# Four transformer stages on one core: the maximum pass of the softmax cut into pairs of units on 64 rows each, with four shared banks

## Chip, core and metric

One NeuronCore of a Trainium2 chip runs the whole program in one launch. The metric is the device time in microseconds; the kernel before has a median of 374.66 us over three runs (373.7 to 376.79).

## What is computed

Two layers work on x of 4 batches x 512 positions x 128 channels, with a context of 154 keys a batch. Each layer is a gated cross attention with a gated feed-forward part behind it; the first feed-forward part is quantised, the second is a recurrence over the batches.

```python
x = x + tanh(g_xattn[0]) * L0_xattn(layernorm(x), ctx, ctx, ...)      # 16 heads of 8
x = x + tanh(g_ffn[0])   * L0_ffn(layernorm(x), ...)                  # 16-bit activations, 4-bit weights
x = x + tanh(g_xattn[1]) * L1_xattn(layernorm(x), ctx, ctx, ...)      # the same with a causal mask
x = x + tanh(g_ffn[1])   * L1_ffn(layernorm(x), ...)                  # c = f*c + i*g, h = tanh(...)
# in both attentions:
attn = softmax(einsum('bhqd,bhkd->bhqk', q, k) / sqrt(8), axis=-1)
out = einsum('bhqk,bhkd->bhqd', attn, v)
```

## The kernel before, in words

**Two passes over the scores.** The softmax takes the exponential of a score less its row's maximum, and scores are computed twice. The maximum pass (`scores_for_top`, L870) computes them with queries on the partitions and keys along the free axis, so that VectorE can reduce over keys (`take_top`, L1184). The negated maxima are split into two parts (`split_top`, L1192), transposed by TensorE (`turn_top`, L894), copied by ScalarE (`copy_top`, L702) and sent by two transfers of the SP queue into spare rows of the query tile. The second pass (`scores`, L903) computes keys x queries, with the maximum subtracted by those rows, ScalarE takes the exponential (`exps`, L709), and `weigh` (L928) multiplies by the values on four strips of 32 columns of the array at once.

**Rows of a tile.** The query tile Q4 has, on its partitions, four blocks j of 32 rows, one for each head of a group g; each block holds the high and low parts of a head's query. Kd is block diagonal in the same way: the keys of head j have only the 32 rows of block j filled. One matmul over 128 rows thus gives up to four heads, each from 32 rows.

**Units.** `max_units` cuts the 64 combinations of query tile (4 of 128 positions) and head (16) of a batch into units that fill a PSUM bank: three heads of 154 keys, 462 columns; in layer 1 the first query tile sees at most 128 keys, and its units are four heads of 128. There are 22 units a batch in layer 0 and 20 in layer 1. A unit that crosses a group of four heads is two matmuls (`parts`). In layer 1 each matmul of the first two query tiles has a mask matmul behind it (L889, an identity times a mask). All these matmuls use the whole array and the type fp32r, one instruction each; fp32 products take two.

**The order of work is written out by hand.** For each layer, i runs from -1 to 4, and each i has 20 slots. In a slot TensorE does one score tile of batch i, then the units that `units_at` gives it (of batch i+1 in slots 0 to 12, first ones of batch i+2 in slots 17 to 19), then what PE_PLAN lists: rounds of `weigh` (slots 7, 10, 13, 17, and the tails at 1 and 3 of the next i), the transposes of normed rows (`turn_normed`, L857), the query projection (`project_q`, L865), `turn_top` at slot 14, the output projection at 8. VectorE and ScalarE follow lists of their own with the same slots. Each engine runs its instructions in order, so a wait stops all that is behind it. At i = -1 there are no score tiles: all units of batch 0 are made, and the first eight of batch 1.

**PSUM.** Two banks are for score tiles, two for the weighted values, three in a ring for units (unit k waits until VectorE has reduced unit k-3), and one, `misc`, for all small products in turn; `fill_misc` waits until the one before has been read out. The feed-forward parts use the same banks under other names.

**Low parts of q.** `q_low` on VectorE computes the low part of the first two batches' queries straight from the bank; at i = -1 the second one stands at slot 6 (SECOND_QLOW_AT).

**Rank-1 bias.** `outputs_x` (L974) adds a bias row by matmuls one row deep (L982), between full matmuls.

## Time and profile before

| | |
|---|---|
| median of three runs | 374.66 us |
| profiled execution: time, span | 375.1 us, 373.0 us |
| TensorE matmuls (PE) | 285.1 us busy, 76% |
| TensorE weight loads (PEld) | 167.8 us, 45% |
| VectorE (DVE) | 251.6 us, 67% |
| ScalarE (ACT) | 182.5 us, 49% |
| GpSimd (POOL) | 125.0 us, 34% |
| mean granted clock of TensorE | 0.897 |
| reductions of the maximum pass (L1188) | 168, 97.2 us |
| matmuls of the maximum pass (L885), masks (L889) | 240, 74.2 us; 48, 13.5 us |
| score matmuls (L913) | 128, 60.2 us |

Busy times are of one profiled execution. The ends of matmuls are modelled in the trace and consecutive ones overlap, so a mean duration of a matmul (383 ns for L885) is more than what it adds to a chain of them; differences between ends show that. The granted clock is a share of full speed: 1.0 is 2.4 GHz, 0.5 is 1.2 GHz.

### The profile page before, as it was taken

The page shows a single profiled execution, that of the slowest core. Times are in us where ns is not written, and L with a number is a line of the kernel's source. Part 1 is how long each engine was busy: PE and PEld are TensorE (multiplying, and loading weights), DVE is VectorE, ACT ScalarE, POOL GpSimd, SP SyncE. Part 2 cuts the span into 40 slices and gives each one's busy share as a digit, 9 for nine tenths or more (in the row PEclk, how much of TensorE's full clock was granted, in tenths as well). Part 3 has the DMA queues.
Part 4 walks back from the last instruction along what each step waited for, and adds up shares of the span by engine and source line. Part 5 has one row for each costly group of instructions (what it writes and reads, how often), then busy time and mean ns, then how long its engine had stood idle before and what let it go on. Part 6 is the DMA issues. An engine that isn't in the chain of part 4 may idle for free. (4 is left out here: it accounts for less than half of the span.)

```text
span 373.0 us, 4445 instructions
## 1 busy us (share of the span) xinstructions
PE 285.1 (76%) x1435; PEld 167.8 (45%) x1435; DVE 251.6 (67%) x529; ACT 182.5 (49%) x295; POOL 125.0 (34%) x263
## 2 busy tenths in 40 slices
PE   0886299899989876985010598799999999999694
PEld 0564154555533244431010586475665755544453
DVE  4788264896955687789989767867586792415413
ACT  1635066556466545669373322246556546463122
POOL 6588860543050301840210139222065013030400
PEclk9969579999999998997555599789999999999989
DMA  8711020020000000000000002201001000000003
GB/s 217 283 72 57 9 84 8 2 91 7 3 7 1 2 0 0 3 0 0 1 0 0 0 0 86 84 35 59 8 30 70 2 0 9 1 0 2 0 0 113
DMA packets 9687, 12.54 MB, mean 34 GB/s; under 512 B 897, under 2 KB 5377, under 8 KB 9665
## 3 DMA queue, kind: packets, MB, share of 16 engines
q1 hardware_dynamic: 9232, 11.80, 8.9%
q10 hardware_dynamic: 432, 0.47, 0.7%
q8 instruction: 11, 0.18, 0.2%
q14 instruction: 12, 0.09, 0.1%
HBM read 4.27 MB, written 1.05 MB: 14 GB/s over the span
## 5 line engine op out<-in xcount | busy, mean ns | idle before, releaser
L1188 DVE TENSOR_REDUCE sb_nm<-ps_top 128x3 f32<-128x462 f32 (+2 forms) x168 | 97.2, 627 | 41.4 <-PE ps_top L885 26.2
L716 ACT ACTIVATE sb_pr<-ps_score 128x512 f32<-128x512 f32 (+1 forms) x160 | 89.6, 584 | 61.9 <-PE ps_score L916 28.1
L885 PE MATMUL ps_top<-sb_Kd,sb_Q 128*128 128x462 f32 (+3 forms) x240 | 74.2, 383 | 7.5 <-DVE sb_nm L1188 2.7
L913 PE MATMUL ps_score<-sb_Q,sb_Kd 128*128 128x512 f32 x128 | 60.2, 482 | 3.4 <-ACT sb_pr L716 3.4
L885 PEld LDWEIGHTS ps_top<-sb_Kd,sb_Q 128*128 128x128 f32 x240 | 44.7, 206 | 23.4 <-DVE sb_nm L1188 14.1
L584 POOL TENSOR_SCALAR sb_var<-sb_mv 128x4 f32<-128x4 f32 x16 | 3.9, 242 | 148.8 <-DVE sb_mv L1151 148.7
L913 PEld LDWEIGHTS ps_score<-sb_Q,sb_Kd 128*128 128x128 f32 x128 | 24.0, 190 | 39.9 <-ACT sb_pr L716 30.9
L945 PE MATMUL ps_pv<-sb_pr,sb_V 128*32 128x512 f32 x256 | 34.1, 605 | 0.0
L1001 PE MATMUL ps_misc<-sb_consts,sb_amx 128*128 128x128 f32 x10 | 3.3, 425 | 31.3 <-DVE sb_amx L1249 29.2
L601 POOL TENSOR_SCALAR sb_xn<-sb_xr,sb_nmean,sb_rstd 128x128 f32<-128x128 f32 x48 | 21.2, 455 | 1.3
L862 PE MATMUL ps_misc<-sb_consts,sb_xn 128*128 128x128 f32 x64 | 11.5, 309 | 12.7 <-POOL sb_xn L601 10.9
L1208 DVE STREAM_TRANSPOSE sb_oq<-ps_pv 128x512 f32<-128x512 f32 x16 | 10.7, 696 | 13.3 <-PE ps_pv L945 13.3
L486 POOL CAST sb_Kd<-sb_K 32x616 fp32r<-32x616 f32 x20 | 13.9, 694 | 11.3 <-ACT sb_xq L797 7.5
L1001 PEld LDWEIGHTS ps_misc<-sb_consts,sb_amx 128*128 128x128 f32 x10 | 2.1, 261 | 33.7 <-DVE sb_amx L1249 32.7
L586 POOL TENSOR_TENSOR sb_rstd<-sb_var,sb_half 128x4 f32<-128x4 f32 x16 | 16.6, 1040 | 1.3
L921 PE MATMUL ps_score<-sb_Q,sb_KT 128*128 128x512 f32 (+1 forms) x32 | 14.6, 472 | 1.7 <-ACT sb_pr L716 1.7
L945 PE MATMUL ps_pv<-sb_pr,sb_VT 128*32 128x512 f32 (+1 forms) x128 | 14.9, 550 | 0.9 <-ACT sb_pr L716 0.9
L862 PEld LDWEIGHTS ps_misc<-sb_consts,sb_xn 128*128 128x128 f32 x64 | 7.9, 156 | 16.0 <-POOL sb_xn L601 12.3
L688 ACT ACTIVATE sb_xnT<-ps_misc 128x512 f32<-128x512 f32 x8 | 4.8, 596 | 21.0 <-PE ps_misc L862 21.0
L1148 DVE BATCH_NORM_STATS2 sb_stat<-sb_xr 128x6 f32<-128x128 f32 x64 | 13.9, 280 | 1.5 <-DMA sb_xr<-x 1.2
L916 PE MATMUL ps_score<-sb_maskr,sb_identr 128*128 128x128 f32 x64 | 14.2, 222 | 0.0
L1077 PE MATMUL ps_score<-sb_xq,sb_wfT 128*128 128x512 f32 x16 | 10.8, 813 | 4.2 <-ACT sb_uf L772 2.3
(162 smaller groups left out, 530.0 us busy)
## 6 DMA issues: line engine op xcount, KB each, us to landing
sb_Q<-sb_qh SPq DMA_DIRECT2D x16, 256.0 KB, 2.3
sb_Q<-sb_ql SPq DMA_DIRECT2D x8, 256.0 KB, 2.3
sb_xr<-x SPq DMA_DIRECT2D x4, 256.0 KB, 8.1
out<-sb_xr SPq DMA_DIRECT2D x4, 256.0 KB, 2.4
sb_wsb<-w SPq DMA_DIRECT2D x1, 704.0 KB, 9.3
sb_wf<-wffn SPq DMA_DIRECT2D x1, 576.0 KB, 9.4
sb_wkr<-wkr SPq DMA_DIRECT2D x2, 256.0 KB, 7.1
sb_Q<-sb_nmT SPq DMA_DIRECT2D x16, 32.0 KB
```

Of the source, the lines that this page charges most:

```text
L486: ins = pool.tensor_copy(Kd[n % 3][q, :, j, :], K4[q, :, b, :])
L586: pool.tensor_tensor(rstd[:, k % 4, :], var[:, k % 4, :], half[:, :], ALU.pow).then_inc(rstd_r, 1)
L601: ins = pool.tensor_scalar(xn[:, kind == "post", t, :], xr[:, TT * b + t, :], nmean[:, k % 4, t:t + 1], rstd[:, k % 4, t:t + 1], ALU.add, ...
L716: act.activation(pr[:, k % PRING, q0:T], score[k % SRING][:, q0:T], ACT.Exp, scale=SCALE).then_inc(exp_r, 1)
L862: ins = pe.transpose(misc[:, P * t:P * t + P], xn[:, kind == "post", t, :], ident[:, :])
L885: ins = pe.matmul(cols[:, c0:c1, :], Q4[n % 3][:, g, P * qt:P * qt + P], Kd[n % 3][:, g, j:j + c1 - c0, 0:keys], start=True, stop=not mask ...
L913: ins = pe.matmul(ps[:, :], Kd[n % 3][:, g, j, 0:P], Q4[n % 3][:, g, :], start=True, stop=(layer == 0), skip_group_check=True)
L916: ins = pe.matmul(ps[:, 0:P], identr[:, :], maskT, start=False, stop=True, skip_group_check=True)
L921: ins = pe.matmul(ps[:, q0:T], KT[:, b, t - H, :], Q4[n % 3][:, t - H, q0:T], start=True, stop=(layer == 0), skip_group_check=True)
L945: ins = pe.matmul(acc[32 * g:32 * g + 32, q0:T], lhs, pr[:, (TILES * n + t) % PRING, q0:T], start=(r in (0, 2)), stop=(r >= 4), skip_group ...
L1148: ins = dve.bn_stats(stat6[:, k % 4, t, :], xr[:, TT * b + t, :])
L1188: dve.tensor_reduce(nm[:, :, :].rearrange("p t h -> p (t h)")[:, f0:f0 + heads], top[k % MRING][:, 0:keys * heads].rearrange("p (h k) -> p ...
```

## The change

The 64 combinations of query tile and head are sorted into two halves: heads of the blocks j = 0, 1 (rows 0 to 63) and heads of the blocks j = 2, 3 (rows 64 to 127). Units come in pairs with the same place in either half, each in a bank of its own. A pair's matmuls alternate between the halves and read 64 rows each, so that every unit of three heads is two matmuls: 42 matmuls a batch instead of 32 in layer 0, 40 instead of 28 in layer 1. Masked pairs have one mask matmul of the whole array for each unit, behind all its parts: 10 a batch instead of 12. `pairs_at` gives whole pairs to slots: at most one in most slots, and none in some that had a unit; the first four pairs of batch 1 are early.

The three banks of units and `misc` become a ring of four, in which units and small products take turns in the written order (`bank_plan`); each waits for the reader of the one that held its bank last (`fill_bank`). Before the slots, and from i = 3 on, small products have the fourth bank alone. The second low part of q moves from slot 6 to slot 4. `split_top` has two instructions for each half. The readers (ScalarE's copies, `q_low`, `residual`) take `shared(...)` for `misc` and are otherwise the same.

```diff
 ROUNDS = 6
 EARLY, LAST = 3, 13
-FIRST_EARLY = 8
+FIRST_EARLY = 4
 PRING = 8
 SRING = 2
-MRING = 3
-FRING = SRING + MRING + 2
+MRING = 4
+LONE = MRING - 1
+FRING = SRING + MRING + 1
...
 
 def max_units(layer):
 
-    units = [(h, J, P) for h in range(0, H, J)] if layer == 1 else []
-    first = H if layer == 1 else 0
-    return units + [(f, min(3, TT * H - f), S) for f in range(first, TT * H, 3)]
+    units = [(half, f, J, P) for f in (0, 4) for half in range(2)] if layer == 1 else []
+    first = 8 if layer == 1 else 0
+    return units + [(half, f, min(3, TT * 8 - f), S) for f in range(first, TT * 8, 3) for half in range(2)]
 
 
 def parts(first, heads):
 
-    cuts = [first] + [f for f in range(first + 1, first + heads) if f % J == 0] + [first + heads]
-    return [(a // H, a % H // J, a % J, a - first, b - first) for a, b in zip(cuts, cuts[1:])]
+    cuts = [first] + [f for f in range(first + 1, first + heads) if f % 2 == 0] + [first + heads]
+    return [(a // 8, a % 8 // 2, a % 2, a - first, b - first) for a, b in zip(cuts, cuts[1:])]
 
 
 UNITS = [max_units(0), max_units(1)]
 CLEAN_MAX_ROWS = (3, 7)
 
 
-def units_at(layer, i, slot):
-
-    n = len(UNITS[layer])
+def pairs_at(layer, i, slot):
+
+    n = len(UNITS[layer]) // 2
     early = lambda b: FIRST_EARLY if b == 1 else n * EARLY // (EARLY + LAST) if b > 1 else 0
     taken = []
     if slot < LAST and 0 <= i + 1 < B:
         first = early(i + 1)
-        taken += [(i + 1, u) for u in range(first + (n - first) * slot // LAST, first + (n - first) * (slot + 1) // LAST)]
+        taken += [(i + 1, p) for p in range(first + (n - first) * slot // LAST, first + (n - first) * (slot + 1) // LAST)]
     if slot >= SLOTS - EARLY and 0 < i + 2 < B:
         k, n = slot - SLOTS + EARLY, early(i + 2)
-        taken += [(i + 2, u) for u in range(n * k // EARLY, n * (k + 1) // EARLY)]
+        taken += [(i + 2, p) for p in range(n * k // EARLY, n * (k + 1) // EARLY)]
...
 SECOND_Q_AT = (-1, 3)
-SECOND_QLOW_AT = (-1, 6)
+SECOND_QLOW_AT = (-1, 4)
...
 
-def misc_plan():
-
-    order = []
+def bank_plan():
+
+    plan = []
     for layer in range(2):
-        order += [(what, layer, b) for b in range(ahead(layer)) for what in ("pre", "q")]
+        plan += [(("pre", layer, 0), LONE), (("q", layer, 0), LONE), (("pre", layer, 1), LONE)]
+        turn = 0
         for i in range(-1, B + 1):
             for slot in range(SLOTS):
-                order += [(what, layer, b) for what, b in planned(PE_PLAN, layer, i, slot) if what in MISC_USERS]
+                names = [("unit", layer, b, 2 * p + half) for b, p in pairs_at(layer, i, slot) for half in range(2)]
+                names += [(what, layer, b) for what, b in planned(PE_PLAN, layer, i, slot) if what in MISC_USERS]
+                if (i, slot) == SECOND_Q_AT:
+                    names.append(("q", layer, 1))
                 if (layer, i, slot) == WEIGHTS_AT:
-                    order += [("w", 0), ("w", 1), ("w", 2)]
+                    names += [("w", k) for k in range(3)]
+                for name in names:
+                    plan.append((name, turn % MRING if i < B - 1 else LONE))
+                    turn += 1
         if layer == 0:
-            for k in range(5):
-                order.append(("gb", k))
-    return order
+            plan += [(("gb", k), LONE) for k in range(5)]
+    return plan
 
 
...
-        nm = sb("nm", [P, TT, H])
+        nm = sb("nm", [P, 2, TT * 8])
...
 
-        misc_uses = misc_plan()
-        use = {name: n for n, name in enumerate(misc_uses)}
+        banks = bank_plan()
+        use = {name: n for n, name in enumerate(name for name, _ in banks if name[0] != "unit")}
+        bank_no = dict(banks)
+        held_by = {}
+        last_in = {}
+        for name, no in banks:
+            held_by[name] = last_in.get(no)
+            last_in[no] = name
+            if name == ("w", 0):
+                last_of_layer = [dict(last_in)]
+        last_of_layer.append(dict(last_in))
+
+        def shared(*name):
+            return top[bank_no[name]]
 
         def misc_read(name):
...
 
-        def fill_misc(pe, name):
-
-            if use[name] > 0:
-                pe.wait_ge(*misc_read(misc_uses[use[name] - 1]))
+        def released(name):
+
+            if name[0] == "unit":
+                return top_red, units_before(B * name[1] + name[2]) + name[3] + 1
+            return misc_read(name)
+
+        def fill_bank(pe, name):
+
+            if held_by[name] is not None:
+                pe.wait_ge(*released(held_by[name]))
+
+        def leave_ring(pe, layer):
+
+            for no in range(LONE):
+                pe.wait_ge(*released(last_of_layer[layer][no]))
 
         def weight(n):
...
-            def scores_for_top(layer, b, u):
-                n = B * layer + b
-                k = units_before(n) + u
-                if u == 0:
+                fill_bank(pe, ("q", layer, b))
+                pe.matmul(shared("q", layer, b)[:, :], weight(WL1 * layer + WQ), xnT[:, :], start=True, stop=True)\
+                    .then_inc(misc_full, 1)
+
+            def scores_for_tops(layer, b, p):
+                n = B * layer + b
+                if p == 0:
                     pe.wait_ge(*q_landed(n))
                     pe.wait_ge(kd_r, n + 1)
                     if n == 0:
                         pe.wait_ge(kd0_r, 1)
-                if k >= MRING:
-                    pe.wait_ge(top_red, k - MRING + 1)
-                f0, heads, keys = UNITS[layer][u]
-                ps = top[k % MRING]
-                cols = ps[:, 0:keys * heads].rearrange("p (h k) -> p h k", h=heads)
+                pair = [UNITS[layer][2 * p + half] for half in range(2)]
+                _, f0, heads, keys = pair[0]
+                masked = max(min(16 - f0, heads), 0) if layer == 1 else 0
+                cols = []
+                for half in range(2):
+                    name = ("unit", layer, b, 2 * p + half)
+                    fill_bank(pe, name)
+                    cols.append(shared(*name)[:, 0:keys * heads].rearrange("p (h k) -> p h k", h=heads))
                 for qt, g, j, c0, c1 in parts(f0, heads):
-                    masked = layer == 1 and qt < 2
-                    ins = pe.matmul(cols[:, c0:c1, :], Q4[n % 3][:, g, P * qt:P * qt + P], Kd[n % 3][:, g, j:j + c1 - c0, 0:keys],
-                                    start=True, stop=not masked, skip_group_check=True)
-                    if masked:
-                        lo = 0 if qt == 0 else P
-                        ins = pe.matmul(cols[:, c0:c1, lo:keys], identr[:, :],
-                                        maskM[:, 0:keys - lo].unsqueeze(1).to_broadcast([P, c1 - c0, keys - lo]),
-                                        start=False, stop=True, skip_group_check=True)
-                ins.then_inc(top_r, 1)
+                    for half in range(2):
+                        rows = slice(64 * half, 64 * half + 64)
+                        j0 = 2 * half + j
+                        ins = pe.matmul(cols[half][:, c0:c1, :], Q4[n % 3][rows, g, P * qt:P * qt + P],
+                                        Kd[n % 3][rows, g, j0:j0 + c1 - c0, 0:keys],
+                                        start=(c0 == 0), stop=(c0 >= masked), skip_group_check=True)
+                        if c1 == heads and masked == 0:
+                            ins.then_inc(top_r[half], 1)
+                if masked > 0:
+                    lo = 0 if keys == P else P
+                    for half in range(2):
+                        pe.matmul(cols[half][:, 0:masked, lo:keys], identr[:, :],
+                                  maskM[:, 0:keys - lo].unsqueeze(1).to_broadcast([P, masked, keys - lo]),
+                                  start=False, stop=True, skip_group_check=True).then_inc(top_r[half], 1)
...
                     pe.wait_ge(c_r, b + 2)
                     pe.wait_ge(top_red, units_before(2 * B))
+                    leave_ring(pe, 1)
...
             def take_top(layer, b, u):
                 k = units_before(B * layer + b) + u
-                f0, heads, keys = UNITS[layer][u]
-                dve.wait_ge(top_r, k + 1)
-                dve.tensor_reduce(nm[:, :, :].rearrange("p t h -> p (t h)")[:, f0:f0 + heads],
-                                  top[k % MRING][:, 0:keys * heads].rearrange("p (h k) -> p h k", h=heads),
+                half, f0, heads, keys = UNITS[layer][u]
+                dve.wait_ge(top_r[half], k // 2 + 1)
+                dve.tensor_reduce(nm[:, half, f0:f0 + heads],
+                                  shared("unit", layer, b, u)[:, 0:keys * heads].rearrange("p (h k) -> p h k", h=heads),
                                   AX.X, ALU.max, negate=True).then_inc(top_red, 1)
 
             def split_top(layer, b):
                 n = B * layer + b
                 dve.wait_ge(top_red, units_before(n + 1))
-                src = nm[:, :, :].rearrange("p t (g j) -> p t j g", g=G)
-                part = [nms[:, :, a, :, :] for a in range(2)]
+                src = [nm[:, half, :].rearrange("p (t g j) -> p t j g", t=TT, g=G) for half in range(2)]
+                part = [[nms[:, :, a, 2 * half:2 * half + 2, :] for half in range(2)] for a in range(2)]
                 if n > 0:
                     dve.wait_ge(nmT_r, n)
-                dve.tensor_copy(part[0], src).then_inc(nmh_r, 1)
-                dve.wait_ge(nmh_r, n + 1)
-                dve.tensor_tensor(part[1], src, part[0].bitcast(F32), ALU.subtract).then_inc(nms_r, 1)
+                for half in range(2):
+                    dve.tensor_copy(part[0][half], src[half]).then_inc(nmh_r, 1)
+                for half in range(2):
+                    dve.wait_ge(nmh_r, 2 * n + half + 1)
+                    ins = dve.tensor_tensor(part[1][half], src[half], part[0][half].bitcast(F32), ALU.subtract)
+                ins.then_inc(nms_r, 1)
 
...
-                        for b, u in units_at(layer, i, slot):
-                            take_top(layer, b, u)
+                        for b, p in pairs_at(layer, i, slot):
+                            take_top(layer, b, 2 * p)
+                            take_top(layer, b, 2 * p + 1)
```

## Rows read from the trace of the kernel before

**Rows 1.** Stages: bounds, length, busy us of PE, PEld, DVE, ACT, POOL; clock; DMA

```profile
48.60:66.40 17.80, 16.89 (x84) 9.04 (x83) 9.79 (x19) 12.23 (x23) 4.62 (x9) 0.95 0.13 48
66.40:89.90 23.50, 21.62 (x124) 11.67 (x123) 19.45 (x49) 13.78 (x26) 11.97 (x23) 1.00 0.10 40
...
266.60:290.90 24.30, 23.57 (x152) 15.20 (x151) 18.54 (x46) 13.87 (x26) 12.01 (x23) 1.00 0.10 38
290.90:312.80 21.90, 20.68 (x139) 13.28 (x137) 15.85 (x36) 12.03 (x23) 4.85 (x11) 1.00 0.01 4
```

**Rows 2.** Timeline of TensorE, layer 0: start us, length us, instructions, their number

```profile
66.70 0.38 PE L885 MATMUL ps_top<-sb_Kd,sb_Q 128*128 128x462 f32 x1
66.92 0.39 PE L913 MATMUL ps_score<-sb_Q,sb_Kd 128*128 128x512 f32 x1
67.15 0.52 PE L885 MATMUL ps_top<-sb_Kd,sb_Q 128*128 128x154 f32 x2
67.60 1.06 PE L945 MATMUL ps_pv<-sb_pr,sb_VT 128*32 128x512 f32 x8
68.59 0.50 PE L913 MATMUL ps_score<-sb_Q,sb_Kd 128*128 128x512 f32 x1
68.93 0.63 PE L885 MATMUL ps_top<-sb_Kd,sb_Q 128*128 128x308 f32 x3
```

**Rows 3.** Waits of weight loads, 48.6 to 111.5: us, times, longest

```profile
PEld ps_score L913 <- ACT sb_pr L716: 10.5, 17, 0.8
PEld ps_top L885 <- DVE sb_nm L1188: 4.8, 12, 0.8
```

**Rows 4.** Timeline of TensorE, layer 0, end of the opening; idle time in brackets

```profile
45.42 1.12 PE L862 MATMUL ps_misc<-sb_consts,sb_xn 128*128 128x128 f32 x4 [6.74 <-POOL sb_xn L601]
```

**Rows 5.** Timeline of VectorE and ScalarE, opening of layer 1

```profile
228.23 3.58 DVE L1188 TENSOR_REDUCE sb_nm<-ps_top 128x4 f32<-128x512 f32 x6 [0.79 <-PE ps_top L889]
...
231.81 0.69 ACT L695 ACTIVATE sb_qh<-ps_misc,sb_cols 128x512 fp32r<-128x512 f32 x1 [5.15 <-PE ps_misc L868]
...
232.19 2.28 DVE L1188 TENSOR_REDUCE sb_nm<-ps_top 128x3 f32<-128x462 f32 x4 [0.38 <-PE ps_top L889]
...
240.62 0.22 DVE L1199 CAST sb_nms<-sb_nm 128x64 fp32r<-128x64 f32 x1
240.87 0.27 DVE L1201 TENSOR_TENSOR sb_nms<-sb_nm,sb_nms 128x64 fp32r<-128x64 f32 x1
```

**Rows 6.** Timeline of TensorE: matmuls one row deep between full ones

```profile
342.68 1.02 PE L971 MATMUL ps_top<-sb_pnT,sb_wsb 128*128 128x512 f32 x2
343.63 0.73 PE L982 MATMUL ps_score<-sb_bfo,sb_onesr 1*128 1x512 f32 x2
344.29 1.16 PE L985 MATMUL ps_score<-sb_wsb,sb_pnT 128*128 128x128 f32 x8
```

**Rows 7.** Timeline of TensorE: eight small matmuls behind a full one

```profile
78.17 0.38 PE L885 MATMUL ps_top<-sb_Kd,sb_Q 128*128 128x462 f32 x1
78.38 1.05 PE L954 MATMUL ps_misc<-sb_wsb,sb_oT 128*128 128x128 f32 x8
```

**Rows 8.** Timeline of TensorE, layer 1: units with masks

```profile
266.81 0.22 PE L916 MATMUL ps_score<-sb_maskr,sb_identr 128*128 128x128 f32 x1
266.88 0.45 PE L885 MATMUL ps_top<-sb_Kd,sb_Q 128*128 128x512 f32 x1
267.16 0.40 PE L889 MATMUL ps_top<-sb_maskr,sb_identr 128*128 128x512 f32 x1
...
269.20 0.23 PE L916 MATMUL ps_score<-sb_maskr,sb_identr 128*128 128x128 f32 x1
...
269.68 0.19 PE L889 MATMUL ps_top<-sb_maskr,sb_identr 128*128 128x52 f32 x1
269.71 0.48 PE L913 MATMUL ps_score<-sb_Q,sb_Kd 128*128 128x512 f32 x1
```

**Rows 9.** Timeline of TensorE: transposes behind ScalarE's copy of the maxima

```profile
85.88 0.44 PE L921 MATMUL ps_score<-sb_Q,sb_KT 128*128 128x512 f32 x1
86.58 0.63 PE L862 MATMUL ps_misc<-sb_consts,sb_xn 128*128 128x128 f32 x4 [0.26 <-ACT sb_nmT L707]
```

More of the change, by code:

```diff
@@ L289, in program @@
         pv = [bank(f"pv{n}") for n in range(2)]
-        misc = bank("misc")
-        fbank = score + top + pv
+        fbank = score + top[0:LONE] + pv
         ybank = score + pv
-        kbank = score + top
+        kbank = score + top[0:LONE]
         dbank = score + pv
@@ L319, in program @@
         m_in = [sem(f"m_in{n}") for n in range(3)]
-        top_r, top_red = sem("top_r"), sem("top_red")
+        top_r = [sem(f"top_r{half}") for half in range(2)]
+        top_red = sem("top_red")
         nmh_r, nms_r, nmT_r = sem("nmh_r"), sem("nms_r"), sem("nmT_r")
@@ L687, in copy_normed @@
                         act.wait_ge(n16_r, B)
-                act.activation(dst, misc[:, :], ACT.Copy).then_inc(xnT_r, 1)
+                act.activation(dst, shared(kind, layer, b)[:, :], ACT.Copy).then_inc(xnT_r, 1)
             def copy_q(layer, b):
@@ L694, in copy_q @@
                     act.wait_ge(*q_landed(n - 2))
-                act.activation(qh[:, n % 2, :], misc[:, :], ACT.Identity,
+                act.activation(qh[:, n % 2, :], shared("q", layer, b)[:, :], ACT.Identity,
                                bias=cols_sb[:, BQ + layer:BQ + layer + 1]).then_inc(qh_r, 1)
@@ L698, in copy_q @@
                     act.wait_ge(ql_r, n)
-                    act.activation(qf[:, :], misc[:, :], ACT.Identity,
+                    act.activation(qf[:, :], shared("q", layer, b)[:, :], ACT.Identity,
                                    bias=cols_sb[:, BQ + layer:BQ + layer + 1]).then_inc(qf_r, 1)
@@ L866, in project_q @@
                 pe.wait_ge(xnT_r, norm_no["pre", layer, b] + 1)
-                fill_misc(pe, ("q", layer, b))
-                pe.matmul(misc[:, :], weight(WL1 * layer + WQ), xnT[:, :], start=True, stop=True).then_inc(misc_full, 1)
-            def scores_for_top(layer, b, u):
+                fill_bank(pe, ("q", layer, b))
+                pe.matmul(shared("q", layer, b)[:, :], weight(WL1 * layer + WQ), xnT[:, :], start=True, stop=True)\
+                    .then_inc(misc_full, 1)
+            def scores_for_tops(layer, b, p):
                 n = B * layer + b
-                k = units_before(n) + u
-                if u == 0:
+                if p == 0:
                     pe.wait_ge(*q_landed(n))
@@ L951, in project_out @@
                 pe.wait_ge(oT_r, n + 1)
-                fill_misc(pe, ("wo", layer, b))
+                fill_bank(pe, ("wo", layer, b))
                 for t in range(TT):
-                    ins = pe.matmul(misc[:, P * t:P * t + P], oT[:, P * t:P * t + P], weight(WL1 * layer + WO),
+                    ins = pe.matmul(shared("wo", layer, b)[:, P * t:P * t + P], oT[:, P * t:P * t + P], weight(WL1 * layer + WO),
                                     start=True, stop=True)
@@ L999, in global_top @@
                 pe.wait_ge(amx_r, k + 1)
-                fill_misc(pe, ("gb", k))
-                pe.matmul(misc[:, 0:P], amx[:, k:k + 1].to_broadcast([P, P]), ident[:, :], start=True, stop=True)\
-                    .then_inc(misc_full, 1)
+                fill_bank(pe, ("gb", k))
+                pe.matmul(shared("gb", k)[:, 0:P], amx[:, k:k + 1].to_broadcast([P, P]), ident[:, :],
+                          start=True, stop=True).then_inc(misc_full, 1)
             def down(c):
@@ L1178, in q_low @@
                     dve.wait_ge(*q_landed(n - 2))
-                dve.scalar_tensor_tensor(out=ql[:, n % 2, :], in0=misc[:, :],
+                dve.scalar_tensor_tensor(out=ql[:, n % 2, :], in0=shared("q", layer, b)[:, :],
                                          scalar=cols_sb[:, BQ + layer:BQ + layer + 1],
```

25 lines of the change are left out of this document (13 added, 12 removed).

## The prediction

> **What bounds the kernel now.** I read the table of stages first [rows 1]. A stage here is one batch's 20 score tiles; next to them TensorE works through the maximum pass of the next batch. In the stages that hold such a pass TensorE shows 16.9 of 17.8, 21.6 of 23.5, 23.6 of 24.3 and 20.7 of 21.9 us busy; VectorE is next with 19.5 of 23.5 and 18.5 of 24.3. The ends of matmuls are modelled, so I check by differences of ends. TensorE's own rows [rows 2] run almost without a hole: a 512-column score ends 0.23 after the matmul before it (67.31 against 67.08), two units of the maximum pass (three matmuls) take 0.47 (69.09 to 69.56), a round of weighted values 0.99. So in these six stages a microsecond more on TensorE is close to a microsecond more of kernel. There is some slack: in the two middle stages of layer 0 weight loads for the maximum pass wait for VectorE to free a bank, 12 times [rows 3]. Elsewhere the pass is hidden or VectorE sets the pace. In layer 0's opening stretch TensorE sits 6.7 us until GpSimd's normed rows come [rows 4]. In layer 1's opening, VectorE runs reductions nearly back to back [rows 5], and before the scores can start their splitting copies must be done.
>
> **The price that decides: changing how the array is cut.** Score tiles use all 128 rows; the new pairs use 64 and 64. The nearest thing in the trace is the rank-1 bias matmul of line 982, one row deep, between full matmuls [rows 6]. L971 ends at 343.70, the two L982 of 512 columns at 344.36: 0.66 where two scores take 0.46, so +0.20 on entering. The eight L985 behind them end at 345.45: 1.09, where the eight equal ones of L954 take 0.88 (78.55 to 79.43, [rows 7]): +0.20 on leaving. The same appears around the 32-column rounds: the score after a round ends 0.43 behind it instead of 0.23 [rows 2], entering costs 0.13. Nothing else is awaited at these places. I take 0.20 each way. The bounds are 0 (the 64-row cut may be no switch from 128, which no row shows) and 0.20. The Trainium skill, TensorEngine Tiling (Array Packing), Key Properties, says that changing the tiling mode, not just the tile, drains the array; by that rule every pair between two scores pays both ways, and the trace agrees for the one-row cut.
>
> **A pair of units.** Before: 0.47 for both [rows 2]. After: each half streams the same 462 columns as one unit did, side by side, in two parts instead of one or two. One unit alone is 0.22 (66.70 to 66.92). A matmul whose predecessor is short waits for its weights: behind the 60 ns mask the next ends 0.29 later, not 0.23 [rows 8], so a load needs about 0.11; with a 154-column part first this adds 0.04 in half the pairs. I take 0.23 a pair, if the two halves' loads also run side by side. The four 32-column tiles of a round do that (eight matmuls in 1.06, [rows 2]); other column strips, though, not other rows. The bounds: side by side, nothing more; one behind the other, 0.1 more on each of the two parts, 0.2 a pair. I take the first, by the nearer row. The same page, Key Properties, says that different tiles load and multiply in parallel; by it the sum stays at 0.23, without it 0.43.
>
> **Counted over the plan.** In the stages with scores, layer 0 has 9+11+9 = 29 pairs; 7 stand right before a round, which switches anyway.
> - 22 pairs: 0.23 + 0.40 - 0.47 = +0.16, +3.5 us. 7 pairs: 0.23 + 0.20 - 0.47 = -0.04, -0.3. Layer 0: **+3.2**.
> - Layer 1 has 7+10+9 = 26. Fifteen unmasked: before 0.47 plus the late weights behind each score's short mask (0.05, 1.3 times a pair) = 0.53; after 0.63, or 0.43 before a round: 10 x 0.10 - 5 x 0.10 = +0.5.
> - Four wholly masked (4 heads x 128 keys): before 2 x 0.53 (267.03 to 267.56, [rows 8]); after 0.20 + 2 x 0.12 + 0.20 + 2 x 0.23 = 1.10: +0.2. Seven of the second query tile: a unit in two parts with two masks takes 0.44 and delays the next score by 0.09 (269.43, 269.87, 270.19, [rows 8]), one in one part about 0.40; together 0.93. After: 0.20 + 0.23 + 0.20 + 2 x 0.11 = 0.85: -0.6 over seven. Slots that now hold no unit let the score's mask delay the next score instead: 4 a stage, +0.5. Layer 1: **+0.6**.
> - Openings. Layer 0: the last two pairs stand behind the wait of 6.7 us [rows 4]; at the lower granted clock two more switches, **+0.3**. The rest, the moved low part of q and its bank, is covered by that wait; without it they would cost 0.6. Layer 1: the first masked pair is ready 0.85 after its start instead of 0.46, while VectorE already waits 0.79 [rows 5]: +0.4. Low q moves ahead of four reductions; VectorE would be at it at 232.2 and the high part is written at 232.50 [rows 5]: +0.3, against 0.4 of waiting there now, so 0. The split becomes four instructions for two, 0.22 and 0.27 now [rows 5]; halves overlap, +0.2. **+0.6**.
> - Four banks in turn. Today the transposes of the normed rows wait for the single small bank until ScalarE has copied the maxima (86.58, [rows 9]), the matmul ending about 0.4 late, in four stages. Another bank removes that, -1.6, but the next score then meets ScalarE's exponentials, which weight loads already await 17 times [rows 3]: I count half, **-0.8**. New waits of the small products on reductions I count at 0: VectorE is seldom more than two units behind; that is a rival below.
> - Slower TensorE shortens VectorE's lag, so some of [rows 3]'s waits vanish: **-0.6**.
>
> Sum: 3.2 + 0.6 + 0.3 + 0.6 - 0.8 - 0.6 = +3.3. The profiled execution took 375.1 (span 373.0); its sum is 378.4. The three timed runs have the median 374.66, 0.44 lower, so I say **378.0**. VectorE's reductions stay 168 of the same sizes; transfers don't change. The granted clock is 1.00 in five of six stages [rows 1]; the pass now asks fewer column times of the array, and I take no fall.
>
> **Rivals.**
> 1. *The 64-row cut is no switch.* Then about 0.40 less on 43 pairs and 0.20 on 12: 19.6 us less on TensorE, -16 against today. VectorE's 19.5 of 23.5 us and the exponential chain stop it about halfway: 375 - 7 = **368**. For it: only a one-row cut is priced in the trace. Against: that cut costs the same as the column cut, both ways. 0.22.
> 2. *Halves take turns* in loading, or in streaming. +0.2 a pair on 55 pairs, 11 us, some 9.5 realised: **388**. It decides against the kernel from any serial cost above 0.01 us a pair. For it: no row-packed load in the trace. 0.16.
> 3. *The shared banks couple TensorE to VectorE.* A transposition or projection now needs a bank that a reduction still holds; the in-order queue behind it, scores included, stops. Price: the waits of the maximum pass for VectorE today, 0.4 each [rows 3]; at 3 of them in each of six stages, less what is hidden, +6: **384**. For it: pairs take two banks at once, so two pairs fill the ring. Against: the bursts are spread over slots. 0.12.
>
> My forecast has 0.50, its own range 376 to 381.5.
>
> **Numbers.** A measurement of this kernel tells about 1% from no change, so the lines are at 370.9 and 378.4. Forecast: 0.30 within, 0.20 above. Rival 1: 0.19 faster, 0.03 within. Rival 2: 0.16 slower. Rival 3: 0.02 within, 0.10 slower. Together faster 0.19, same 0.35, slower 0.46. The range takes in most of rivals 1 and 2: 368.5 to 387.
>
> **What would show it.** Right: a pair's two first parts start within some ns of each other; the first ends 0.20 later than its columns explain; the score behind a pair ends about 0.43 after it. The six stages together come out about 3 us longer, layer 0 carrying most. Rival 1: that score ends 0.23 after the pair. Rival 2: the second half's matmul ends 0.1 or more behind the first's. Rival 3: waits of transposes and projections for reductions in the list of waits. Wrong altogether if the granted clock falls in a stage that has 1.00 now: at the lower level every matmul there doubles its columns' time, several us a stage.

## The result, and the profile after

The changed kernel took 390.5 us in the median of four runs (385.0, 385.8, 395.2, 398.6) against 375.65 beside it: slower. Its runs fall into a group near 385 and one from 395 up, and every ratio in this document compares a kernel's lower group with that of the kernel before. Here it is **1.026, interval 1.019 to 1.033**, about 385 us: clearly above 1, while whether the loss exceeds 2% stays open. My forecast was 378.0 with a range to 387, and slower its likeliest sign; the amount was three times too small, and most of the causes were others.

The trace taken with this result is of a run of 395.2 us. The windows of its six score stages, which answer to [rows 1] (bounds, length, busy us of PE, PEld, DVE, ACT, POOL, then granted clock, DMA):

```profile
51.40:72.80 21.40, 20.49 (x92) 8.72 (x90) 9.52 (x21) 12.60 (x23) 4.58 (x9) 0.76 0.10 40
72.80:97.00 24.20, 21.97 (x134) 10.11 (x132) 19.78 (x51) 14.00 (x26) 12.03 (x23) 1.00 0.10 39
97.00:119.40 22.40, 19.53 (x120) 8.77 (x119) 17.77 (x41) 12.15 (x23) 4.85 (x11) 1.00 0.01 5
261.50:284.80 23.30, 21.61 (x110) 11.74 (x109) 8.66 (x19) 12.48 (x23) 4.60 (x9) 0.78 0.10 38
284.80:309.80 25.00, 23.73 (x161) 13.61 (x160) 19.28 (x48) 13.55 (x25) 12.01 (x23) 1.00 0.10 37
309.80:333.70 23.90, 21.39 (x150) 12.13 (x148) 18.04 (x39) 11.58 (x22) 4.82 (x11) 1.00 0.01 3
```

Every stage is longer, the first of each layer most, and there the clock is 0.76 and 0.78. A second execution of the same kernel (span 384.6; I call it the repeat) has the first stages at 0.94 and 0.96:

```profile
51.50:70.20 18.70, 17.70 (x92) 7.53 (x90) 9.41 (x21) 12.59 (x23) 4.61 (x9) 0.94 0.12 46
...
257.00:276.30 19.30, 17.87 (x110) 10.10 (x109) 7.79 (x18) 12.26 (x23) 4.61 (x9) 0.96 0.12 46
```

The first stage is 4.0 us shorter there in layer 1 and 2.7 in layer 0. The code is the same and the other four stages have the same lengths in both traces, so that difference is the clock. All comparisons of stretches below use the repeat.

TensorE's timeline after, layer 0, answers to [rows 2]:

```profile
79.55 0.48 PE L952 MATMUL ps_score<-sb_Q,sb_Kd 128*128 128x512 f32 x1
79.95 0.52 PE L921 MATMUL ps_top<-sb_Kd,sb_Q 64*128 64x154 f32 x4
80.40 0.50 PE L952 MATMUL ps_score<-sb_Q,sb_Kd 128*128 128x512 f32 x1
```

The score ends at 80.03, the pair's four matmuls (two of 154 columns, two of 308) at 80.47, the next score at 80.90. The single records show the first two parts ending at 80.289 and 80.293, the second two at 80.466 and 80.470: side by side within 4 ns. The first ends 0.266 after the score; its 154 columns take 0.064 at 2.4 GHz, which leaves 0.20 for entering. The score behind the pair ends 0.43 after it, 0.20 more than a score behind another full matmul. Each of my three numbers for the cut (0.20 in, 0.23 for a pair, 0.20 out) is there. The first matmul of a round ends 0.547 behind a pair, as it did behind whole units.

Ends of the openings. For [rows 4] the transposes of the normed rows start at 47.68 (45.42 before) and TensorE waits 5.1 us for them instead of 6.7. For [rows 5], layer 1's reductions now wait for the masked pairs, and the low part of q of batch 1 stands ahead of the others:

```profile
47.68 1.11 PE L893 MATMUL ps_top<-sb_consts,sb_xn 128*128 128x128 f32 x4 [5.09 <-POOL sb_xn L631]
```

```profile
238.77 1.29 DVE L1228 TENSOR_REDUCE sb_nm<-ps_top 128x4 f32<-128x512 f32 x2 [1.04 <-PE ps_top L929]
240.29 1.29 DVE L1228 TENSOR_REDUCE sb_nm<-ps_top 128x4 f32<-128x512 f32 x2 [0.23 <-PE ps_top L929]
241.76 1.19 DVE L1228 TENSOR_REDUCE sb_nm<-ps_top 128x3 f32<-128x462 f32 x2 [0.18 <-PE ps_top L929]
244.55 0.75 DVE L1219 SCALAR_TENSOR_TENSOR sb_ql<-ps_top,sb_cols,sb_qh 128x512 fp32r<-128x512 f32 x1 [1.60 <-ACT sb_qh L725]
```

Six reductions ran behind one wait of 0.79 before; now they run two at a time behind waits of 1.04, 0.23 and 0.18, and VectorE waits 1.60 before the low part of q, which I had put at nothing. For [rows 9], the transposes behind the copy of the maxima run at once (93.04, no bracket). The waits over the whole execution that bear on rival 3 (us, times, longest; the first line is of the kernel before):

```profile
PE ps_misc L899 <- DVE sb_nms L1201: 3.0, 2, 1.5
...
PEld ps_top L938 <- DVE sb_nms L1243: 9.1, 7, 2.1
...
PE ps_top L938 <- DVE sb_nms L1243: 7.0, 6, 1.8
...
PE ps_top L993 <- DVE sb_nm L1228: 1.8, 2, 1.1
...
PE ps_top L893 <- DVE sb_ql L1219: 0.6, 1, 0.6
```

L938 is the transposition of the split maxima (L899 before): 7.0 us of waiting for 3.0. The last two are the only waits of small products for a reader of a unit or of q's low part: 2.4 us, of which 0.8 was there before.

### The profile page after: what moved, and what is told of

It reads as the page before. It is cut to its first block and busy times, and to the rows that moved or that the text cites. A ratio compares the mean times of both kernels' runs of the same rounds, so it can differ in the third digit from the quotient of the medians.

```text
span 393.1 us, 4712 instructions
## 1 busy us (share of the span) xinstructions
PE 298.4 (76%) x1515; PEld 163.7 (42%) x1515; DVE 253.5 (64%) x545; ACT 182.3 (46%) x295; POOL 124.6 (32%) x263
## 5 line engine op out<-in xcount | busy, mean ns | idle before, releaser
L952 PE MATMUL ps_score<-sb_Q,sb_Kd 128*128 128x512 f32 x128 | 63.3, 527 | 3.6 <-ACT sb_pr L746 3.6
L921 PE MATMUL ps_top<-sb_Kd,sb_Q 64*128 64x308 f32 (+2 forms) x328 | 50.3, 392 | 10.7 <-DVE sb_nm L1228 4.1
L921 PEld LDWEIGHTS ps_top<-sb_Kd,sb_Q 64*128 64x128 f32 x328 | 31.2, 232 | 35.3 <-DVE sb_nm L1228 18.6
L984 PE MATMUL ps_pv<-sb_pr,sb_V 128*32 128x512 f32 x256 | 36.6, 646 | 0.0
L1041 PE MATMUL ps_top<-sb_consts,sb_amx 128*128 128x128 f32 x10 | 3.3, 425 | 31.3 <-DVE sb_amx L1292 29.2
L631 POOL TENSOR_SCALAR sb_xn<-sb_xr,sb_nmean,sb_rstd 128x128 f32<-128x128 f32 x48 | 21.4, 458 | 1.3
L1251 DVE STREAM_TRANSPOSE sb_oq<-ps_pv 128x512 f32<-128x512 f32 x16 | 10.7, 696 | 13.8 <-PE ps_pv L984 13.8
L893 PE MATMUL ps_top<-sb_consts,sb_xn 128*128 128x128 f32 x64 | 11.5, 309 | 9.5 <-POOL sb_xn L631 8.9
L1041 PEld LDWEIGHTS ps_top<-sb_consts,sb_amx 128*128 128x128 f32 x10 | 2.1, 261 | 33.7 <-DVE sb_amx L1292 32.7
L725 ACT ACTIVATE sb_qh<-ps_top,sb_cols 128x512 fp32r<-128x512 f32 x8 | 5.5, 687 | 19.0 <-PE ps_top L899 19.0
L718 ACT ACTIVATE sb_xnT<-ps_top 128x512 f32<-128x512 f32 x8 | 4.8, 596 | 20.1 <-PE ps_top L893 20.1
L955 PEld LDWEIGHTS ps_score<-sb_maskr,sb_identr 128*128 128x128 f32 x64 | 13.0, 204 | 1.3 <-issue 1.2
```

What stands on the lines that cost most here:

```text
L631: ins = pool.tensor_scalar(xn[:, kind == "post", t, :], xr[:, TT * b + t, :], nmean[:, k % 4, t:t + 1], rstd[:, k % 4, t:t + 1], ALU.add, ...
L893: ins = pe.transpose(shared(kind, layer, b)[:, P * t:P * t + P], xn[:, kind == "post", t, :], ident[:, :])
L921: ins = pe.matmul(cols[half][:, c0:c1, :], Q4[n % 3][rows, g, P * qt:P * qt + P], Kd[n % 3][rows, g, j0:j0 + c1 - c0, 0:keys], start=(c0 = ...
L952: ins = pe.matmul(ps[:, :], Kd[n % 3][:, g, j, 0:P], Q4[n % 3][:, g, :], start=True, stop=(layer == 0), skip_group_check=True)
L955: ins = pe.matmul(ps[:, 0:P], identr[:, :], maskT, start=False, stop=True, skip_group_check=True)
L984: ins = pe.matmul(acc[32 * g:32 * g + 32, q0:T], lhs, pr[:, (TILES * n + t) % PRING, q0:T], start=(r in (0, 2)), stop=(r >= 4), skip_group ...
```

## The experiments

All but the first are the changed kernel with one or two things undone or moved. Ratios are to the kernel before on the same chip. **Repeat** is the changed kernel itself.

> The changed kernel once more, for a second look at its trace. Both theories: about 385 us in an undisturbed run. Clock theory: the length follows the time that TensorE spends at the lower granted clock around the two openings and the first score stages; a run with a mean clock near 0.88 is near 385, one near 0.84 is near 395. Switch theory alone: the same length whatever the clock does in the first score stages, within 1 us.

390.7 median (385.7 to 398.6). Its four runs have mean granted clocks of 0.871, 0.867, 0.843 and 0.832 at 386.7, 385.7, 394.7 and 398.6 us: the two long runs have the lower clock, as the clock theory wanted.

**All 128 rows everywhere.** A pair's matmuls read the whole tile (P is 128); pairs, slots, banks and masks stay.

```diff
-                        rows = slice(64 * half, 64 * half + 64)
+                        rows = slice(0, P) if True else slice(64 * half, 64 * half + 64)
```

> The changed kernel, but each matmul of the maximum pass reads all 128 rows again (the key tile is block diagonal, so the result is the same): no side by side, no switch of the cut; pairs, plan of slots and the four shared banks stay. Switches and clock (my theory): both costs go, 374 to 378 us. Shared banks couple TensorE to VectorE (rival): nothing of that goes, 383 us or more, since the matmuls take longer than side by side.

383.8 (381.6 to 387.1), ratio 1.022 (1.016 to 1.028). Nearly the whole loss is there without any 64-row cut. My account of the loss fell here; the cut's own share, 0.4%, is inside the intervals.

**128 rows in the openings only**, and **in the stages only** (`rows` by `i < 0`).

> All 128 rows in the openings only (batch 0 and the first four pairs of batch 1 of each layer), 64 and 64 rows next to the score tiles. Clock theory: the openings keep TensorE at the higher clock as in the kernel before, the switches of the stages stay: 377 to 380 us, and the first score stages fall back to about 18.5 and 19.5 us. If the clock doesn't hang on the openings: 384 to 386.

> 64 and 64 rows in the openings only, all 128 rows next to the score tiles. Clock theory: the openings still drop the clock and the first score stages start at the lower one: 379 to 383 us; without the switches the four later stages are as before within 0.5 us each. Switch theory alone: 375 to 377.

384.2, 1.023 (1.018 to 1.028), and 384.3, 1.020 (1.014 to 1.026). Neither can be told from the other or from the two ends. The switches that I had counted at 3 us aren't found in the time.

**Why they aren't.** I went through layer 0's second stage slot by slot, from one score's end to the next. A slot with one pair takes 0.87 in the repeat and 0.74 with all rows (slots 5, 11), about as worked out. But slots 0, 4, 6, 12 and 14 come out at 0.31, 2.24, 1.66, 0.97 and 1.45 against 0.45, 2.32, 1.80, 1.04 and 1.52: 0.50 less in all. In each of them TensorE waits for another engine, and the wait shrinks by what the pairs in front of it grew (in 0 for an exponential, in 4 for GpSimd's normed rows, in 6 for ScalarE's copy of the transposes, in 12 for a reduction, in 14 for VectorE's split maxima). Slots 7 and 10, whose pair stands before a round, gain 0.05 each (1.84 and 1.83 against 1.89 and 1.88), near the 0.04 of my count. Before the last slot the repeat is 0.05 ahead, where eight pairs away from rounds, at 0.13 each, would put it 1.0 behind; over the whole stage it is 0.10 behind. The six stages together differ by 1.2 us (table below).

**The small products with the fourth bank alone**, units in the other three; with row pairs, and with all 128 rows:

```diff
-                for name in names:
-                    plan.append((name, turn % MRING if i < B - 1 else LONE))
-                    turn += 1
+                for name in names:
+                    if name[0] == "unit":
+                        plan.append((name, turn % LONE))
+                        turn += 1
+                    else:
+                        plan.append((name, LONE))
```

> The changed kernel, row pairs kept, but the small products (transposes, projections) have the fourth bank alone again, and the units take turns in the other three. Theory now: in the shared ring a small product's bank ties TensorE's in-order queue to VectorE; in layer 0's opening the second low part of q holds a ring bank, the pair behind it waits, and the values matmuls, the tail keys and GpSimd's normed rows come 2 to 3 us late. By this the kernel falls from 385 to 379 to 381: layer 0's first score back from 51.5 to 48.6 to 49.5, the stages 1 to 2 us shorter in sum. Rival (pairs as the unit of work: two banks at a time, bursts of two pairs, empty slots): the coupling stays or grows with a ring of three, 384 to 387. Rival (switches of the array's cut alone): no change, 385.

> All 128 rows everywhere and the small products alone in their bank; still planned pair by pair, masks merged. The shared-bank theory: 375 to 377.5, since nothing is left but the plan of slots. The pair-plan rival: 381 to 384, like the kernel with all 128 rows and the shared ring (383.8).

402.8, 1.068 (1.062 to 1.074), and 397.6, 1.056 (1.049 to 1.063). My second account (small products in the ring) had the wrong sign: the ring of four is what makes pairs bearable. In the first of the two the pairs' waits for banks are TensorE's longest:

```profile
PEld ps_top L924 <- DVE sb_nm L1231: 40.9, 58, 1.5
...
PE ps_top L924 <- DVE sb_nm L1231: 21.5, 35, 1.2
```

(L924 is the pair's matmul there, L1231 the reduction; before, the first was 14.1 us.) A pair needs two of three banks at once, so it can hardly run ahead of VectorE.

**Single units**, in the slots of the kernel before, all 128 rows: with the small bank alone and the low part of q back in slot 6, and with the shared ring of four and the low part in its new slot 4. (In the shared ring it can't go back to slot 6: TensorE would wait for that low part to be read out of its bank while VectorE, in order, still waits for a unit behind it, and neither would go on. That variant has no time.)

```diff
-FIRST_EARLY = 4
+FIRST_EARLY = 8
...
-    n = len(UNITS[layer]) // 2
+    n = len(UNITS[layer])
...
-                        for b, p in pairs_at(layer, i, slot):
-                            scores_for_tops(layer, b, p)
+                        for b, u in pairs_at(layer, i, slot):
+                            scores_for_top(layer, b, u)
```

> As the one before, but units are planned one by one in the slots of the kernel before, and the second low part of q is back in its slot. Left of the change: the units' cut into two heads by two (more two-part units), one mask a unit, four short splitting copies. Every theory: 374 to 376. If it is at 378 or more, the two-part units or the masks cost what I put down to banks and plan.

> All 128 rows, units planned and issued one by one; the four banks are still shared in turns with the small products, one mask a unit, second low part of q in its new slot. My first account (the small products in the ring, the low part of q first of all, hold TensorE back) wants 380 or more here. The account that stands after the kernels with the small bank apart (402.8 and 397.6 with pairs, 373.9 with single units): it is the pair that costs, two banks at once out of few; then this is 372 to 376.

373.9, 0.995 (0.991 to 0.999), and **372.8, 0.991 (0.988 to 0.995)**: both are a little faster than the kernel before, by 0.5% and 0.9%. One mask a unit, more two-part units, the four splitting copies and the ring cost nothing together. The whole loss is in the pairs.

**One after the other.** All 128 rows, the pairs' slots, but each unit waits for its own bank only and is released at its own end.

```diff
                 for half in range(2):
                     name = ("unit", layer, b, 2 * p + half)
                     fill_bank(pe, name)
...
+                    for qt, g, j, c0, c1 in parts(f0, heads):
                         j0 = 2 * half + j
+                        ins = pe.matmul(cols[:, c0:c1, :], Q4[n % 3][:, g, P * qt:P * qt + P],
+                                        Kd[n % 3][:, g, j0:j0 + c1 - c0, 0:keys],
                                         start=(c0 == 0), stop=(c0 >= masked), skip_group_check=True)
...
+                    ins.then_inc(top_r[half], 1)
```

> The kernel with all 128 rows at 383.8, with one thing changed: the two units of a pair come one behind the other, each awaiting only its own bank and released to VectorE at its own end; slots, banks and masks stay those of the pairs. If it is taking two banks at once that costs: 375 to 378. If it is where the plan puts them (two units in one slot, none in the next, up to four in the last slot of an opening): 381 to 384. Between the two, the parts can be read off.

378.3, 1.008 (1.004 to 1.011). It lies between, and the intervals on both sides are apart: taking two banks at once costs 1.4% (1.022 against 1.008), the pairs' slots 1.6% (1.008 against 0.991). The first share also holds that the matmuls of a pair alternate, so that its first unit is ready late; no run separates the two.

**Single units in the openings**, row pairs in the stages.

> The changed kernel with its row pairs in the stages, but in the two openings single units on all 128 rows, in the slots of the kernel before. From the traces, 5 to 5.5 of its 11 us arise before the first scores of the two layers: then 379 to 381, with layer 0's first score back at 48.6 to 49.3 from 51.5, and the stages unchanged (24.2 and 22.4 us, 25.0 and 23.9 in layer 1). Rival: the opening's delay is the second low part of q in the ring, which stays: first score at 50.5 or later, 383 to 385.

383.4, 1.022 (1.016 to 1.027): outside what I wrote. Its openings did what was expected: the first score is at 48.9, and from layer 0's last score to layer 1's first 119.3 us pass where the repeat takes 124.3. But the clock fell inside layer 1's first stage:

```profile
248.90:272.10 23.20, 21.51 (x110) 11.76 (x109) 8.30 (x18) 12.47 (x23) 4.58 (x9) 0.78 0.10 38
```

23.2 us at 0.78 against 19.3 at 0.96 in the repeat. Without these 3.9 us it would be at 379.5, where expected; that is worked out, not run.

**The pass one slot earlier.** `EARLY, LAST = 3, 12` for `3, 13`: first in the changed kernel, then in the one at 372.8.

> The changed kernel with one number changed: the pairs of the maximum pass are spread over the first 12 slots of a stage instead of 13. In the traces planned by pairs, in layer 1's second and third stage, six reductions stand back to back before VectorE splits the maxima (four in the kernel before), and the transposes of the split maxima, with the scores queued behind them, wait 1.1 to 1.4 us. If that is the stages' loss: these two stages get 0.8 to 1.2 us shorter each (25.0 to 24.0, 23.9 to 22.8), layer 0's 0 to 0.5 each, the kernel 381 to 383. Rival (the loss in the stages is the switches of the cut or the masks): stages unchanged, 384 to 386. Where the granted clock falls in another place, the stages tell it and the total does not.

> The kernel that beat the one before (372.8: all 128 rows, single units, shared ring of four, one mask a unit), with the units over the first 12 slots. The wait before the transposes of the maxima is 0.3 to 0.6 there, in four stages: 371.5 to 373. Rival (fuller slots push the scores behind ScalarE and VectorE earlier in the stage): 373 to 375, and 13 slots stay the better number.

The first took 390.9 (388.4 to 391.2 in four runs), 1.037 (1.031 to 1.044), slower, yet its stages did what was expected and more: 25.0 to 24.0 and 23.9 to 21.5 in layer 1, 22.4 to 21.9 in layer 0's third. All of it and more went to the clock, in layer 1's first stage:

```profile
258.20:284.20 26.00, 25.51 (x117) 14.52 (x116) 9.12 (x20) 12.69 (x23) 4.58 (x9) 0.66 0.09 34
```

The second came to 0.993 (0.989 to 0.998), which can't be told from 0.991. Ten of its twelve runs took 371.3 to 377.9 us, the other two 508 and 1,426; nothing here explains these two. So 13 slots and 372.8 us stand as the best version.

## Where the 11.6 us went

Spans between the same events (first units, first score of each batch), each from one trace; the kernel before has span 373.0.

| stretch, us | before | repeat | all rows | one after other | single units, ring of 4 |
|---|---|---|---|---|---|
| to layer 0's first score | 48.6 | 51.5 | 50.8 | 49.4 | 48.9 |
| its three stages | 62.9 | 65.3 | 65.0 | 64.6 | 63.0 |
| last stage, feed-forward, to the first unit of layer 1 | 116.0 | 117.2 | 116.4 | 114.8 | 116.2 |
| layer 1's opening | 20.2 | 23.0 | 21.1 | 20.2 | 19.9 |
| its three stages | 65.1 | 68.2 | 67.3 | 66.9 | 65.0 |
| the rest | 60.2 | 59.4 | 59.4 | 60.3 | 59.4 |
| span | 373.0 | 384.6 | 380.0 | 376.2 | 372.4 |

Read from right to left the columns take the loss apart. The six stages: the pairs' slots 3.5 us (128.0 to 131.5), two banks at once 0.8 (to 132.3), 64 rows 1.2 (to 133.5). The two openings: the slots 0.8 us, two banks 2.3, 64 rows together with the clock 2.6. The stretch behind layer 0's stages, most of it feed-forward with code that doesn't differ, takes 114.8 to 117.2 in these five traces, which nothing here explains; a difference of a microsecond in one stretch that isn't at full clock is therefore not safe.

**The stages: a late split.** They are 5.5 of the 11.6, and the largest part is the plan of slots. Whole pairs give slots 9 to 12 of layer 1's later stages 0, 2, 2, 2 units, where single ones were 2, 1, 1, 2. VectorE in layer 1's second stage, before:

```profile
282.62 2.24 DVE L1188 TENSOR_REDUCE sb_nm<-ps_top 128x3 f32<-128x462 f32 x4
284.90 0.26 DVE L1199 CAST sb_nms<-sb_nm 128x64 fp32r<-128x64 f32 x1
285.19 0.28 DVE L1201 TENSOR_TENSOR sb_nms<-sb_nm,sb_nms 128x64 fp32r<-128x64 f32 x1
```

and the same place in the repeat, with GpSimd and TensorE:

```profile
291.52 3.33 DVE L1228 TENSOR_REDUCE sb_nm<-ps_top 128x3 f32<-128x462 f32 x6
294.89 0.71 DVE L1240 CAST sb_nms<-sb_nm 128x32 fp32r<-128x32 f32 x2
...
295.11 1.69 POOL L599 TENSOR_TENSOR sb_xg<-sb_xr,sb_bog 128x128 f32<-128x128 f32 x4
...
295.52 0.92 DVE L1243 TENSOR_TENSOR sb_nms<-sb_nm,sb_nms 128x32 fp32r<-128x32 f32 x2
...
296.49 0.61 PE L938 MATMUL ps_top<-sb_consts,sb_nms 128*32 128x128 f32 x4 [1.09 <-DVE sb_nms L1243]
```

Six reductions stand ahead of the split instead of four, 1.1 us. The four splitting instructions then fall beside GpSimd's residual addition (L599) and take 1.6 us. With single units the same four take 0.70 (L1232 and L1235 there, from 285.19, beside GpSimd's L631, which reads one tensor). TensorE's queue stands 1.09 at L938, with the scores behind it: that slot takes 2.00 us instead of 0.90, and in the next stage 2.07 instead of 0.90. These two slots are 2.3 of layer 1's 3.1. In layer 0 the 2.4 us are not traced to a slot. With the pass one slot earlier, four reductions stand there, the four splitting instructions take 0.67, and L938 doesn't wait (the two stages are 1.0 and 2.4 us shorter, layer 0's three together 0.6):

```profile
299.22 2.24 DVE L1228 TENSOR_REDUCE sb_nm<-ps_top 128x3 f32<-128x462 f32 x4
301.49 0.32 DVE L1240 CAST sb_nms<-sb_nm 128x32 fp32r<-128x32 f32 x2
301.76 0.35 DVE L1243 TENSOR_TENSOR sb_nms<-sb_nm,sb_nms 128x32 fp32r<-128x32 f32 x2
```

The trace shows the slow ones beside a GpSimd instruction with two tensor inputs, and the quick ones beside one with a single tensor input (L631). Instruction by instruction, the slow four end at 295.18, 295.60, 296.02 and 296.44, each 0.03 to 0.05 us after one of GpSimd's (295.15, 295.57, 295.98, 296.39). The Trainium skill, SBUF — State Buffer, SBUF: two separate sides, says that VectorE and GpSimd share one pair of ports as an exclusive lock, held for a whole instruction, which two inputs from SBUF on VectorE's side also claim. The trace agrees for the subtractions (L1243) beside L599, about 0.50 each. The casts, with one input, are as slow. Beside L631, which reads SBUF too, with the pass one slot earlier, the first subtraction took 0.25 and ended 0.04 us after one of GpSimd's; the second took 0.18, as where GpSimd was idle. Why VectorE gets its turn there and not beside L599, the trace doesn't say. No run here takes GpSimd's work away, so the lock itself is argued.

**Layer 0's opening: the cover was hung on what it covered.** It is 2.9 us longer, 2.2 with all 128 rows. The second low part of q now has a ring bank, and the next pair waits for it; behind the pair, in order, stand the values matmuls (L885 after). With all 128 rows:

```profile
28.19 1.19 PE L921 MATMUL ps_top<-sb_Kd,sb_Q 128*128 128x308 f32 x4 [1.77 <-DVE sb_ql L1219]
29.18 1.99 PE L885 MATMUL ps_pv<-sb_wsb,sb_ctx 128*128 128x128 f32 x8
```

Before (L854 there):

```profile
26.81 1.05 PE L854 MATMUL ps_pv<-sb_wsb,sb_ctx 128*128 128x128 f32 x8
```

ScalarE's two copies of the values start 3.3 and 2.8 us later (31.21 and 34.76, for 27.90 and 31.96), GpSimd's normed rows start at 45.08 for 43.63 (45.92 in the repeat), and TensorE's transposes at 46.88 for 45.42 (47.72). Single units with the same ring and the same slot of q wait there too, 1.47, but VectorE, which had waited less for units, reads the low part at 25.92 and not at 27.30, and the values matmuls run at 27.03; the first score is at 48.9. So it needs the pair. That the low part's bank is what matters is read from this chain and not tested by itself. The other 0.7 us can't be given to the 64 rows: with 128 rows in both openings the first score came at 51.9 in one kernel and at 50.8 in the other, with a granted clock of 0.55 and 0.62 from the first unit on (0.55 in the repeat, 0.68 in the kernel before).

**The clock.** Granted clock in layer 1's opening, first unit to first score:

```profile
227.50:247.70 20.20, 17.54 (x73) 11.99 (x73) 16.71 (x30) 4.62 (x7) 7.59 (x12) 0.83 0.11 43
```

before; in the repeat:

```profile
234.00:257.00 23.00, 18.48 (x87) 11.52 (x87) 17.28 (x33) 4.62 (x7) 7.62 (x12) 0.66 0.10 38
```

Before, the clock is 2.4 GHz until 238.2 and then 1.2 for 6.8 us; in the repeat it is 1.2 for 17.1 us (241.4 to 258.4). TensorE was busy 9.5 of the 10.7 us ahead of the fall before, 6.2 of 7.4 in the repeat. Over the kernels, that stretch at 1.2 GHz lasted 6.8 us with single units on all rows (before and three others), 10.2 to 13.7 with pairs on all 128 rows there (four kernels), 17.1 to 34.1 where the opening had row pairs (repeat, the trace at 395, three others). With single units in the opening and row pairs in the stages it was 10.2, and 10.2 more in the first stage. It goes on while TensorE is wholly busy: in the kernel with the pass one slot earlier it ran from 241.6 to 275.7, TensorE busy in all of its last 25.7 us. The pair's switches hardly cost time in a stage at full clock; what they seem to cost in and behind an opening is this. It is shown as a pattern over kernels in layer 1's opening, not by an experiment on the clock alone, and layer 0's opening doesn't keep to it (above).

## Why the prediction was right or wrong

- **The price of the cut, the pair side by side**: right, each number to 0.01 us. Rivals 1 and 2 are out by the ends of matmuls. That the time lies inside my range is luck: its upper end, 387, was put there for rival 2, and my forecast's own range ended at 381.5.
- **"A microsecond more on TensorE is close to a microsecond more of kernel"**: the premise that failed first. +3.2 and +0.6 for the stages rested on it; between all rows and row pairs the six stages differ by 1.2 us (0.3 in layer 0, 0.9 in layer 1, part of it the clock in its first stage). A score ends 0.23 after the matmul before it wherever TensorE isn't waiting, but some slots wait for another engine (in the stage above each time for another one), and those take the extra time back. I read the busy share and the rows without a hole, and passed over the waits in my own [rows 3] and [rows 9].
- **The stages grew by 5.5, for other reasons**, 3.5 of it with the pairs' slots. "VectorE's reductions stay 168 of the same sizes" is true and missed the point: their order against the split changed. I had the pairs per slot and counted switches with them; I did not follow VectorE's queue to slot 13 and ask what stands ahead of the split. Layer 1, which I gave 0.6, got 3.1; layer 0, 3.2 against 2.4.
- **Layer 0's opening, "covered by that wait; without it they would cost 0.6"**: wrong, 2.9 (2.2 with all rows). The wait for GpSimd was not independent of TensorE: it hangs on the values matmuls in the same in-order queue.
- **Layer 1's opening, +0.6**: 2.8 in the repeat; in it are the masked pairs' waits (1.04 for 0.79, then 0.4 more), 1.60 before the low part of q that I had cancelled against another wait, and the clock. With all rows it is 0.9, so 1.9 came with the 64 rows and the longer stretch at 1.2 GHz; these two no run separates.
- **Four banks, -0.8**: the sign was right. The ring is worth 0.3% with single units (0.995 against 0.991, not separable) and 3.4% with pairs (1.056 against 1.022).
- **Rival 3, 384 us at 0.12** came nearest in number. Its waits, small products for reductions, are 2.4 us over the execution, not 6; the sentence "pairs take two banks at once" beside it was one mechanism, worth 1.4%, and I had used it only as support. The other, the pairs' slots, worth 1.6%, stood in none of my rivals.
- **"I take no fall" of the clock**: wrong in the openings, and in the trace at 395 also in both first stages, 2.7 and 4.0 us. I had named it as what would make the forecast wrong altogether, and gave it no chance.

## What to carry to other kernels

Before pricing instructions on the busiest engine, list its own waits in that stretch: extra work ahead of a wait is free up to the wait's length. Making the unit of planning coarser is a change of its own: write down, for each consumer's queue, what now stands ahead of the one step on which the next stage hangs, and how many buffers a step takes at once out of how many. And a wait that is named as cover must be followed back to its start; if it hangs on the queue that is being delayed, it covers nothing.

## What the runs showed of the hardware

- Going from 128-row tiles to a pair of 64-row tiles and back costs 0.20 us each way at 2.4 GHz, as a one-row cut does; matmuls on the upper and lower 64 rows run at once: in the repeat's stages 102 of 106 such couples end within 8 ns of each other, the rest within 35.
- Two copies and two subtractions of 128 x 32 took 0.67 us beside a GpSimd instruction with one tensor input, and 1.63 beside one with two.
- A stretch of TensorE at 1.2 GHz can last 34 us, the last 26 of them with TensorE wholly busy; the first stage of layer 1 took 18.9, 19.3, 23.3 and 26.0 us at granted clocks of 1.00, 0.96, 0.78 and 0.66 (the kernel before, the repeat, the trace at 395, the pass one slot earlier).
